# A graph-network kernel on one core: a step's five quads of edge sums spread between the other TensorE work, the first steps reordered, the looks at dst's order moved into the loop

## The chip, the cores and the metric

The kernel runs on 1 core of a Trainium2 chip. The metric is the device time in microseconds (us) of one launch; lower is better. Engines: PE is TensorE, DVE is VectorE, ACT is ScalarE, POOL is GpSimd, SP is SyncE (here it only issues DMAs).

## What is computed

12500 nodes with 128 features, 412500 edges with 48 features, sorted by receiving node dst. The reference, cut:

```python
h   = relu(layernorm(x))                                   # 12500 x 128
agg = segment_sum(edge_attr_48, dst, 12500)                # 12500 x 48
u   = graph_globals[0]                                     # 64, the same for all nodes
hid = relu(concat([h, agg, u], axis=1) @ W1 + b1)          # 12500 x 256
out = x + hid @ W2 + b2                                    # 12500 x 128
```

## The kernel before, in words

**Tiling.** Edges are read in groups of 896 (128 partitions x 7), 19 groups to a step; 24 full steps and a short one of 5 groups make 25 steps. Nodes are taken in 25 tiles of 512. Because dst is sorted, step s touches about the nodes of tile s. The 19 groups are five quads (QUADS, four groups each, the last three), in two parts: part 0 is quads 0 to 2, part 1 quads 3 and 4 (PART_QUADS).

**Sums of edges.** `make_onehot` (L795, VectorE) compares each edge's node relative to its group with a ramp of 32. `sum_quad` (L1042, TensorE) multiplies a quad's one-hots with its edges, 28 matmuls per four-group quad and pass, and leaves sums in group_bank[part]; its last matmul signals edges_used, which lets SP load the same quad of the next step (`load_quad`, L343) and VectorE make its next one-hots. `copy_sums` (ScalarE, L586) copies the sums (high part), `low_sums` (VectorE, L831) takes what is left (low part), and `place` (TensorE, L1064) places both in a window of nodes with a mask from `make_placing` (VectorE, L807). `add_window` (VectorE, L824) adds the window to agg in SBUF.

**Node network.** `moments`, `join_moments`, `invert` (VectorE, L840, L846, L853, L855) and `deviate`, `normalise` (ScalarE, L593, L601) normalise a tile of x; `turn_x` (TensorE, L1081) transposes it; `copy_turned` (ScalarE, L612) copies it. For the edge part of the first layer, `tile_high` (ScalarE, L623) copies a tile of agg and `tile_low` (GpSimd, L536) subtracts; tile s-1 is complete once part 0 of step s is added, so tile_high(s-1) waits for add_window(s, 0). `first_layer` (L1091 node, L1095 and L1097 edge matmuls) needs both; `relu_hidden` (ScalarE, L633), `second_layer` (L1108), `copy_out` (ScalarE, L641), `add_out` (GpSimd, L531) follow, the latter with `x_plus_b2` (GpSimd, L519). out_bank is used by the second layer and by turn_x in turn, hidden_bank by the first layer and by turn_rel.

**Order.** Each engine has its own program in order; semaphores join them. In step s TensorE does quads 0 to 2, second layer of tile s-2, place part 0, quads 3 and 4, turn x of tile s, first layer of tile s-1, place part 1. VectorE's and ScalarE's orders are written out in the loops of L911 and L689. GpSimd does x_plus_b2(s), tile_low(s-1), add_out(s-2). SP loads all quads of the next step, then x two tiles ahead, and every second step from 4 on stores a tile; the other stores stand at the end. All these DMAs are in one queue.

**rel.** dst is loaded in four blocks of 128 groups. `relative` (ScalarE, L562, L565) makes each row relative, `turn_rel` (TensorE, L1027) transposes it into hidden_bank, `copy_rel` (ScalarE, L574) copies it out; blocks 1 to 3 are turned in steps 2 to 4. `turn_places` (L1115) makes the positions for the masks in step 0. `sum_bias` (L1123) and `bias` (ScalarE, L671) make the hidden bias in step 1.

**The end.** `check_sorted` (VectorE, L750) looks over a block of dst for a descent, four times; `check_windows` tests the windows; a worst value decides whether a general path runs (it does not with these inputs). `last_out` (L869) adds the last two tiles.

## Time and profile before

| | us |
|---|---|
| median of 3 runs | 273.01 (272.47 to 273.25) |
| profiled execution | 272.62 |
| its span, first to last instruction | 270.9 |
| busy: PE, DVE, ACT, POOL | 243.4, 229.1, 144.7, 104.1 |
| DMA | 94.48 MB, mean 349 GB/s |

The profiled execution's time is its span and 1.7 us around it. Times in rows count from the span's start. Matmuls overlap: the starts of following groups tell the time that they take, not their busy sums, and ends of matmuls are modelled.

### The profile page before, as it was taken

Reading aid. Unit: us, or ns where it says so; the run is one execution under the profiler, and the core shown is the slowest. Engines: PE = TensorE matmul, PEld = TensorE weight load, DVE = VectorE, ACT = ScalarE, POOL = GpSimd, SP = SyncE. Lnnn points to the kernel's source line nnn. Section 1 sums busy time; section 2 is a strip of 40 time slices with the busy share of each in tenths; the row PEclk is TensorE's granted clock in tenths of the full one; section 3 lists DMA queues with packets and bytes.
Section 4 is the critical chain, followed back from the end, with each engine's and each line's share of the span. In section 5 each row is a group of like instructions: output and inputs, shape, how many; then the busy total and the mean of one; then the engine's idle time right before and its main releaser. Section 6 shows DMA issues by size and latency. Waiting matters only on the chain.

```text
span 270.9 us, 17352 instructions
## 1 busy us (share of the span) xinstructions
PE 243.4 (90%) x7438; PEld 198.7 (73%) x7438; DVE 229.1 (85%) x556; ACT 144.7 (53%) x315; POOL 104.1 (38%) x112
## 2 busy tenths in 40 slices
PE   6646599999999989999998999998999998999990
PEld 3545578878977877787786788787779678778760
DVE  1967987898999998989999899998989988985294
ACT  2644456966764555466465455536537546545540
POOL 8761033253255235225415514532532550552400
PEclk9977799999999999999999999999999999999996
DMA  7999989999999999999999999999999999999911
GB/s 242 370 359 354 341 277 374 339 328 361 341 377 377 387 384 381 367 380 382 366 385 384 388 373 371 389 382 385 381 359 364 387 382 390 362 387 322 372 48 55
DMA packets 70873, 94.48 MB, mean 349 GB/s; under 512 B 4324, under 2 KB 64260, under 8 KB 70854
## 3 DMA queue, kind: packets, MB, share of 16 engines
q1 hardware_dynamic: 69802, 94.29, 98.5%
q10 hardware_dynamic: 956, 0.00, 0.2%
q14 instruction: 15, 0.12, 0.1%
q8 instruction: 4, 0.07, 0.1%
q0 software_dynamic: 96, 0.00, 0.0%
HBM read 87.88 MB, written 6.40 MB: 348 GB/s over the span
## 4 chain that ended last, share of the span: by engine, by line
PE 46%; DMA 38%; DVE 9%; issue 3%; POOL 1%; DVEq 1%; ACT 0%; POOLq 0%
DMA edge_buf<-in_edge_attr 36%; PE group_bank L1042 18%; PE out_bank L1108 9%; PE hidden_bank L1091 8%; PE window_bank L1064 3%; DVE onehot L795 3%; PE out_bank L1081 3%; PE hidden_bank L1095 2%; PE hidden_bank L1097 2%; PE hidden_bank L1027 2%; DVE rel_rows L750 1%; DMA dst_rows<-in_dst 1%; DVE placing L807 1%; DVE bn L840 1%; DVEq L815 1%
## 5 line engine op out<-in xcount | busy, mean ns | idle before, releaser
L795 DVE TENSOR_TENSOR onehot<-rel,const_bank 128x896 f32<-128x896 f32 (+1 forms) x122 | 122.8, 1023 | 8.2 <-issue 7.9
L1042 PE MATMUL group_bank<-edge_buf,onehot 128*32 128x48 f32 x6454 | 90.2, 213 | 7.4 <-DMA edge_buf<-in_edge_attr 5.8
L1042 PEld LDWEIGHTS group_bank<-edge_buf,onehot 128*32 128x32 f32 x6454 | 81.9, 114 | 14.4 <-issue 9.8
L536 POOL TENSOR_TENSOR tile_sums<-agg,tile_sums 48x512 fp32r<-48x512 f32 x23 | 29.2, 1268 | 137.4 <-ACT tile_sums L623 137.4
L1108 PE MATMUL out_bank<-w_sb,hidden 128*128 128x128 f32 x384 | 48.5, 279 | 1.7 <-issue 0.9
L1108 PEld LDWEIGHTS out_bank<-w_sb,hidden 128*128 128x128 f32 x384 | 44.7, 191 | 4.1 <-issue 1.3
L1091 PE MATMUL hidden_bank<-normed_t,w_node 128*128 128x512 f32 (+1 forms) x100 | 46.4, 586 | 0.4 <-ACT hidden L633 0.4
L601 ACT ACTIVATE normed_x<-x_buf,shift,inverse 128x128 f32<-128x128 f32 x98 | 40.3, 494 | 2.0 <-DVE shift L855 2.0
L633 ACT ACTIVATE hidden<-hidden_bank,hidden_bias 128x512 f32<-128x512 f32 (+1 forms) x50 | 31.2, 676 | 10.7 <-PE hidden_bank L1097 10.7
L519 POOL TENSOR_TENSOR xb_buf<-x_buf,b_rows 128x512 f32<-128x512 f32 (+1 forms) x25 | 31.6, 1262 | 7.9 <-DMA x_buf<-in_x 4.7
L593 ACT ACTIVATE deviation<-mean_var,eps_col 128x4 f32<-128x4 f32 (+1 forms) x25 | 7.4, 298 | 48.3 <-DVE mean_var L846 48.3
L824 DVE TENSOR_TENSOR agg<-agg,window_bank 48x352 f32 (+1 forms) x49 | 21.6, 441 | 13.4 <-PE window_bank L1064 13.2
L531 POOL TENSOR_TENSOR out_buf<-mlp_out,xb_buf 128x512 f32<-128x512 f32 x23 | 29.3, 1275 | 5.6 <-ACT mlp_out L641 3.9
L641 ACT ACTIVATE mlp_out<-out_bank 128x512 f32<-128x512 f32 x23 | 13.7, 597 | 31.2 <-PE out_bank L1108 31.2
L1095 PE MATMUL hidden_bank<-tile_sums,w_high 112*128 112x512 f32 (+1 forms) x50 | 29.0, 581 | 0.1
L1064 PE MATMUL window_bank<-placing,sums_high 128*48 128x128 f32 (+3 forms) x122 | 23.4, 250 | 4.8 <-DVE sums_low L831 3.5
L1091 PEld LDWEIGHTS hidden_bank<-normed_t,w_node 128*128 128x128 f32 x100 | 17.0, 190 | 12.5 <-issue 12.3
L807 DVE TENSOR_TENSOR placing<-node_ramp,const_bank 128x456 fp32r<-128x456 f32 (+2 forms) x49 | 24.9, 508 | 0.0
L623 ACT ACTIVATE tile_sums<-agg 48x512 fp32r<-48x512 f32 (+1 forms) x25 | 15.6, 625 | 12.6 <-DVE agg L824 9.7
L1064 PE MATMUL window_bank<-placing,sums_low 128*48 128x128 f32 (+3 forms) x122 | 21.7, 233 | 0.0
L840 DVE BATCH_NORM_STATS2 bn<-x_buf 128x6 f32<-128x128 f32 x98 | 21.0, 271 | 0.0
L1064 PEld LDWEIGHTS window_bank<-placing,sums_high 128*48 128x48 f32 (+1 forms) x122 | 15.4, 126 | 6.5 <-issue 5.4
(97 smaller groups left out, 217.4 us busy)
## 6 DMA issues: line engine op xcount, KB each, us to landing
edge_buf<-in_edge_attr SPq DMA_DIRECT2D x97, 672.0 KB, 7.4
edge_buf<-in_edge_attr SPq DMA_DIRECT2D x24, 504.0 KB, 8.1
x_buf<-in_x SPq DMA_DIRECT2D x24, 256.0 KB, 8.3
out<-out_buf SPq DMA_DIRECT2D x23, 256.0 KB, 5.8
dst_rows<-in_dst SPq DMA_DIRECT2D x3, 448.5 KB, 6.7
dst_rows<-in_dst SPq DMA_DIRECT2D x1, 252.3 KB
out<-out_buf SPq DMA_DIRECT2D x1, 224.0 KB
edge_buf<-in_edge_attr SPq DMA_DIRECT2D x1, 168.0 KB, 5.7
```

The source lines that it names most:

```text
L519: pool.tensor_tensor(xb_buf[k.third][:, 0:nj, :], x_buf[k.parity][:, 0:nj, :], b2_rows[:, :].unsqueeze(1).to_broadcast([P, nj, F_NODE]), A ...
L531: pool.tensor_tensor(out_buf[slot(k)][:, 0:nj, :], mlp_out[:, 0:nj, :], xb_buf[k.third][:, 0:nj, :], ALU.add).then_inc(out_added, 1)
L536: pool.tensor_tensor(sums_tile(k, STACK_LOW), agg_tile(k), sums_tile(k, 0).bitcast(fp32), ALU.subtract)\
L601: done = act.activation(normed_x[:, j, :], x_buf[k.parity][:, j, :], ACT.Relu, bias=shift[:, j:j + 1], scale=inverse[:, j:j + 1])
L633: act.activation(hidden[own(k)][:, c, 0:cols], hidden_bank[c][:, 0:cols], ACT.Relu, bias=hidden_bias[:, c:c + 1]).then_inc(hidden_copied, 1)
L795: dve.tensor_tensor(onehot[:, c0:c0 + cols, :], rel[:, r0:r0 + cols].unsqueeze(2).to_broadcast([P, cols, WINDOW]), ramp_const.unsqueeze(1) ...
L807: dve.tensor_tensor(placing[h][:, 0:nq, :, 0:width], node_ramp[:, :, 0:width].unsqueeze(1).to_broadcast([P, nq, NJ, width]), position_cons ...
L1042: done = pe.matmul(group_bank[h][WINDOW * j:WINDOW * (j + 1), n * F_EDGE:(n + 1) * F_EDGE], onehot[:, (g0 + j) * EDGES_PER_ROW + r, :], ed ...
L1064: done = pe.matmul(bank[:, :, low // NJ:high // NJ], sums[h][0:rows, n, :], placing[h][0:rows, n, :, 0:(high - low) // NJ], start=(n + par ...
L1091: pe.matmul(hidden_bank[c][:, 0:cols], w1_node[:, c * P:(c + 1) * P], normed_t[own(k)][:, 0:cols], start=True, stop=False)
L1095: pe.matmul(hidden_bank[c][:, 0:cols], w1_high[:, c * P:(c + 1) * P], tile_sums[own(k)][:, 0:cols], start=False, stop=False)
L1108: done = pe.matmul(to_bank[:, j * P:(j + 1) * P], hidden[own(k)][:, c, j * P:(j + 1) * P], w2_sb[:, c, :], start=(c == 0), stop=(c == 1))
```

## The change

On TensorE a step becomes: quads 0 and 1, second layer (and in steps 1 to 3 turn_rel of block s), quads 2 and 3, turn x, place part 0, quad 4, first layer with place part 1 between its node and its edge matmuls. VectorE takes the moments ahead of part 0's low sums and part 1's low sums ahead of the fourth one-hot. ScalarE copies the result and rel ahead of part 0's sums. The first steps load x sooner, and the bias loads have a semaphore of their own; the other weights come behind the last quad of step 1. The low part of w1 is made by GpSimd. check_sorted runs in steps 10, 13, 16 and 19. Cut of the diff:

```diff
@@ -183,6 +183,7 @@
         bases_in = sem("bases_in")
         weights_in = sem("weights_in")
         b2_in = sem("b2_in")
+        bias_in = sem("bias_in")
         edges_in = [sem(f"edges_in{q}") for q in range(NQ)]
         x_in = [sem(f"x_in{p}") for p in range(2)]
         stored = [sem(f"stored{n}") for n in range(OUT_SLOTS)]
@@ -379,23 +380,23 @@
                 for row in (0, STACK_LOW):
                     sp.dma_start(w1_edge[row:row + F_EDGE, :], w1[F_NODE:F_NODE + F_EDGE, :])\
                         .then_inc(weights_in, 16)
-                sp.dma_start(w1_global[:, :], w1[F_NODE + F_EDGE:, :]).then_inc(weights_in, 16)
-                sp.dma_start(global_col[:, :], graph_globals[0:1, :].rearrange("a g -> g a")).then_inc(weights_in, 16)
-                sp.dma_start(b1_col[:, :], b1.rearrange("(c p) -> p c", p=P)).then_inc(weights_in, 16)
                 sp.dma_start(w1_node[:, :], w1[0:F_NODE, :]).then_inc(weights_in, 16)
                 sp.dma_start(w2_sb[:, :, :], w2.rearrange("(c p) n -> p c n", p=P)).then_inc(weights_in, 16)
 
             load_dst(0)
             load_part(At(0), 0)
+            load_x(At(0))
             load_part(At(0), 1)
-            load_x(At(0))
             sp.dma_start(b2_rows[:, :], bass.AP(tensor=b2.tensor, offset=0, ap=[[0, P], [1, F_NODE]]))\
               .then_inc(b2_in, 16)
             load_part(At(1), 0)
             load_x(At(1))
-            load_weights()
+            sp.dma_start(w1_global[:, :], w1[F_NODE + F_EDGE:, :]).then_inc(bias_in, 16)
+            sp.dma_start(global_col[:, :], graph_globals[0:1, :].rearrange("a g -> g a")).then_inc(bias_in, 16)
+            sp.dma_start(b1_col[:, :], b1.rearrange("(c p) -> p c", p=P)).then_inc(bias_in, 16)
             load_dst(1)
             load_part(At(1), 1)
+            load_weights()
             load_dst(2)
             load_x(At(2))
             for s in range(1, steps):
@@ -538,6 +539,12 @@
 
             for s in range(steps):
                 x_plus_b2(last_tile() if s == tiles - 1 else At(s))
+                if s == 1:
+                    pool.wait_ge(xb_ready, s + 1)
+                    pool.wait_ge(w1_high_ready, 1)
+                    pool.tensor_tensor(w1_low[:, :], w1_edge[:, :], w1_high[:, :].bitcast(fp32), ALU.subtract)\
+                        .then_inc(w1_split, 1)
+                    pool.wait_ge(w1_split, 1)
                 if 1 <= s < full_steps:
                     pool.wait_ge(xb_ready, s + 1)
                     tile_low(At(s - 1))
@@ -661,7 +668,7 @@
                    .then_inc(agg_zeroed, 1)
 
             def split_weights():
-                act.wait_ge(weights_in, 7 * 16)
+                act.wait_ge(weights_in, 4 * 16)
                 act.wait_ge(stacks_zeroed, 3)
                 act.activation(w1_high[:, :], w1_edge[:, :], ACT.Copy).then_inc(w1_high_ready, 1)
 
@@ -677,32 +684,33 @@
             act.sem_inc(turned_copied, 1)
             act.sem_inc(bias_ready, 1)
             zero_strip(2)
-            copy_sums(At(0), 0)
             zero_strip(3)
             deviate(At(0))
             normalise(At(0))
+            copy_sums(At(0), 0)
+            copy_turned(At(0))
             copy_sums(At(0), 1)
-            copy_turned(At(0))
-            split_weights()
+            bias()
+            relative(1)
             deviate(At(1))
             normalise(At(1))
             for s in range(1, full_steps):
                 following = last_tile() if s + 1 == tiles - 1 else At(s + 1)
+                if s >= 2:
+                    copy_out(At(s - 2))
+                if s < blocks:
+                    copy_rel(s)
                 copy_sums(At(s), 0)
                 if s == 1:
-                    bias()
-                if s >= 2:
-                    copy_out(At(s - 2))
-                if 2 <= s <= blocks:
-                    copy_rel(s - 1)
+                    split_weights()
                 tile_high(At(s - 1))
                 copy_sums(At(s), 1)
                 deviate(following)
                 relu_hidden(At(s - 1))
                 copy_turned(At(s))
                 normalise(following)
-                if s < blocks:
-                    relative(s)
+                if s + 1 < blocks:
+                    relative(s + 1)
                 if s == 2 * blocks:
                     load_ends(1)
             third, second, last = At(tiles - 3), At(tiles - 2), last_tile()
@@ -886,50 +894,47 @@
             for q in (3, 4):
                 make_onehot(At(0), q)
             make_onehot(At(1), 0)
-            low_sums(At(0), 0)
+            moments(At(0))
+            join_moments(At(0))
+            make_onehot(At(1), 1)
+            invert(At(0))
+            step_bases()
+            base = [window_base(At(0), h) for h in range(2)]
             dve.wait_ge(position_turned, 1)
             dve.tensor_copy(position_const.rearrange("p q s -> p (q s)"), out_bank[:, 0:NQ * steps])\
                .then_inc(position_ready, 1)
             make_placing(At(0), 0)
-            moments(At(0))
-            join_moments(At(0))
+            low_sums(At(0), 0)
             make_placing(At(0), 1)
-            make_onehot(At(1), 1)
-            invert(At(0))
-            step_bases()
-            base = [window_base(At(0), h) for h in range(2)]
             make_onehot(At(1), 2)
-            low_sums(At(0), 1)
             dve.wait_ge(agg_zeroed, 4)
             add_window(At(0), 0, base[0])
+            low_sums(At(0), 1)
             make_placing(At(1), 0)
             make_onehot(At(1), 3)
             moments(At(1))
             join_moments(At(1))
             make_onehot(At(1), 4)
             invert(At(1))
+            check_steps = [2 * blocks + 2 + 3 * b for b in range(blocks)]
             for s in range(1, full_steps):
                 n = At(s + 1)
                 add_window(At(s - 1), 1, base[1])
                 make_placing(At(s), 1)
-                if s == 1:
-                    dve.wait_ge(w1_high_ready, 1)
-                    dve.tensor_tensor(w1_low[:, :], w1_edge[:, :], w1_high[:, :].bitcast(fp32), ALU.subtract)\
-                       .then_inc(w1_split, 1)
                 if n.value * GROUPS % P + GROUPS > P:
                     dve.wait_ge(rel_ready, 2 * (n.value * GROUPS // P + 2))
                 make_onehot(n, 0)
                 base[0] = window_base(At(s), 0)
                 make_onehot(n, 1)
+                following = last_tile() if s + 1 == tiles - 1 else n
+                moments(following)
+                join_moments(following)
                 low_sums(At(s), 0)
                 make_onehot(n, 2)
                 add_window(At(s), 0, base[0])
                 make_placing(n, 0)
+                low_sums(At(s), 1)
                 make_onehot(n, 3)
-                low_sums(At(s), 1)
-                following = last_tile() if s + 1 == tiles - 1 else n
-                moments(following)
-                join_moments(following)
                 base[1] = window_base(At(s), 1)
                 make_onehot(n, 4)
                 invert(following)
@@ -938,6 +943,8 @@
                     c0 = first_last * EDGES_PER_ROW
                     link(dve.memset(rel[0:masked_rows, c0:c0 + EDGES_PER_ROW], -1.0))
                     link(dve.memset(rel[0:masked_rows + 1, c0:c0 + masked_rest], -1.0))
+                if s in check_steps:
+                    check_sorted(check_steps.index(s))
             second, last = At(tiles - 2), last_tile()
             base[0] = window_base(At(steps - 1), 0)
             add_window(At(full_steps - 1), 1, base[1])
@@ -946,8 +953,6 @@
             dve.wait_ge(tile_low_ready, tiles - 2 + 2)
             tile_low(second)
             tile_low(last)
-            for b in range(blocks):
-                check_sorted(b)
             check_windows()
             last_out(second, out_bank, tiles - 1)
             last_out(last, group_bank[0], tiles)
@@ -1081,7 +1086,7 @@
                     done = pe.transpose(to_bank[:, j * P:(j + 1) * P], normed_x[:, j, :], ident[:, :])
                 done.then_inc(x_turned, 1)
 
-            def first_layer(k):
+            def first_layer(k, between=None):
                 pe.wait_ge(w1_split, 1)
                 pe.wait_ge(bias_ready, 3)
                 pe.wait_ge(turned_copied, k.value + 2)
@@ -1090,6 +1095,8 @@
                     pe.wait_ge(hidden_copied, k.value * 2 + c + 5)
                     pe.matmul(hidden_bank[c][:, 0:cols], w1_node[:, c * P:(c + 1) * P], normed_t[own(k)][:, 0:cols],
                               start=True, stop=False)
+                if between is not None:
+                    place(between, 1)
                 pe.wait_ge(tile_low_ready, k.value + 3)
                 for c in range(2):
                     pe.matmul(hidden_bank[c][:, 0:cols], w1_high[:, c * P:(c + 1) * P], tile_sums[own(k)][:, 0:cols],
@@ -1117,7 +1124,7 @@
                 done.then_inc(position_turned, 1)
 
             def sum_bias():
-                pe.wait_ge(weights_in, 7 * 16)
+                pe.wait_ge(bias_in, 3 * 16)
                 pe.wait_ge(rel_ready, 2)
                 for c in range(2):
                     done = pe.matmul(hidden_bank[c][:, 0:1], w1_global[:, c * P:(c + 1) * P], global_col[:, :],
@@ -1140,25 +1147,31 @@
             keep_clock(4, window_bank[0])
             with pe.Fori(0, full_steps) as i:
                 step = At(0, i)
-                sum_part(step, 0)
-                with pe.If(i > blocks):
+                sum_quad(step, 0)
+                sum_quad(step, 1)
+                with pe.If(i >= blocks):
                     second_layer(step.plus(-2))
                 with pe.Else():
                     with pe.If(i > 1):
                         second_layer(step.plus(-2))
-                        turn_rel(i - 1)
+                        turn_rel(i)
                     with pe.Else():
                         with pe.If(i > 0):
-                            sum_bias()
+                            pe.wait_ge(bias_ready, 3)
+                            turn_rel(1)
                         with pe.Else():
                             turn_places()
+                sum_quad(step, 2)
+                sum_quad(step, 3)
+                turn_x(step)
                 place(step, 0)
-                sum_part(step, 1)
-                turn_x(step)
+                sum_quad(step, 4)
                 with pe.If(i > 0):
-                    pe.wait_ge(rel_ready, i * 2)
-                    first_layer(step.plus(-1))
-                place(step, 1)
+                    pe.wait_ge(rel_ready, i * 2 + 2)
+                    first_layer(step.plus(-1), step)
+                with pe.Else():
+                    sum_bias()
+                    place(At(0), 1)
 
             final, third, second, last = At(steps - 1), At(tiles - 3), At(tiles - 2), last_tile()
             sum_part(final, 0)
```

## Rows read from the trace of the kernel before

**Rows 1.** The page, GB/s moved in 40 equal slices of the span (6.8 us each).
```profile
GB/s 242 370 359 354 341 277 374 339 328 361 341 377 377 387 384 381 367 380 382 366 385 384 388 373 371 389 382 385 381 359 364 387 382 390 362 387 322 372 48 55
```
**Rows 2.** Chain of waits that ended last: start us, duration us, what.
```profile
47.92 0.24 PE window_bank L1064 x4
...
78.06 1.92 PE group_bank L1042 x168
...
82.05 0.41 PE window_bank L1064 x6
82.47 1.32 PE group_bank L1042 x98
83.79 0.59 PE out_bank L1081 x4
84.37 1.72 PE hidden_bank L1091 x4
86.09 0.23 PE hidden_bank L1095
...
87.27 1.33 PE group_bank L1042 x112
...
128.29 8.79 DMA edge_buf<-in_edge_attr
```
**Rows 3.** Timeline, from placing part 0 to tile_low, and a late first-layer matmul.
```profile
179.01 0.24 PE L1064 MATMUL window_bank<-placing,sums_low 128*48 128x152 f32 x1
...
179.39 0.52 DVE L824 TENSOR_TENSOR agg<-agg,window_bank 48x352 f32 x1 [0.52 <-PE window_bank L1064]
...
179.94 0.63 ACT L623 ACTIVATE tile_sums<-agg 48x512 fp32r<-48x512 f32 x1 [0.46 <-DVE agg L824]
...
180.71 1.27 POOL L536 TENSOR_TENSOR tile_sums<-agg,tile_sums 48x512 fp32r<-48x512 f32 x1 [5.69 <-ACT tile_sums L623]
...
257.44 1.05 DVE L861 TENSOR_TENSOR tile_sums<-agg,tile_sums 48x512 fp32r<-48x512 f32 x2 [0.76 <-ACT tile_sums L623]
...
258.21 0.50 PE L1095 MATMUL hidden_bank<-tile_sums,w_high 112*128 112x512 f32 x1
```
**Rows 4.** VectorE: timeline of a step, line L855 (ns min/median/max), and GpSimd beside it.
```profile
78.70 0.36 DVE L824 TENSOR_TENSOR agg<-agg,window_bank 48x216 f32 x1
...
83.04 0.61 DVE L807 TENSOR_TENSOR placing<-node_ramp,const_bank 128x456 fp32r<-128x456 f32 x1
...
87.92 0.37 DVE L824 TENSOR_TENSOR agg<-agg,window_bank 48x216 f32 x1
...
L855 DVE SCALAR_TENSOR_TENSOR shift<-mean_var,inverse x25: 161/732/986, 20.0 to 251.0; 128x4 f32<-128x4 f32 x24, 128x2 f32<-128x2 f32 x1
...
173.73 1.29 POOL L519 TENSOR_TENSOR xb_buf<-x_buf,b_rows 128x512 f32<-128x512 f32 x1
...
174.31 0.73 DVE L855 SCALAR_TENSOR_TENSOR shift<-mean_var,inverse 128x4 f32<-128x4 f32 x1
```
**Rows 5.** Timeline of ScalarE in steps 2 and 3, where blocks of rel are turned.
```profile
42.63 1.87 ACT L574 ACTIVATE rel<-hidden_bank 128x512 f32<-128x512 f32 x2
...
47.56 1.26 ACT L633 ACTIVATE hidden<-hidden_bank,hidden_bias 128x512 f32<-128x512 f32 x2 [0.31 <-PE hidden_bank L1097]
...
50.96 1.04 ACT L565 ACTIVATE rel_rows<-dst_rows,neg_first 128x896 f32<-128x896 int32 x1
```
**Rows 6.** Timeline of TensorE: first sums of step 2 and of the final step.
```profile
37.76 0.42 PE L1042 MATMUL group_bank<-edge_buf,onehot 128*32 128x48 f32 x20
...
252.25 1.38 PE L1042 MATMUL group_bank<-edge_buf,onehot 128*32 128x48 f32 x70
```
**Rows 7.** Timeline of the end.
```profile
258.52 1.09 DVE L750 CUSTOM_DVE_ANT_0 rel_rows<-dst_rows 128x896 f32<-128x896 int32 x1
...
263.10 1.06 PE L1108 MATMUL group_bank<-w_sb,hidden 128*128 128x128 f32 x8
...
266.67 0.41 DVE L869 TENSOR_TENSOR out_buf<-group_bank,xb_buf 128x256 f32<-128x256 f32 x1
```

## The prediction

> **What bounds it now.** I read the page's slices first, then the chain of waits, then the timeline of single steps. The slices of GB/s [rows 1] stand at 242 to 374 in the first third and near 380 from then until the loop ends: the edges come in at the best rate the run shows, and the early shortfall is made by the kernel. The chain says who holds the loop. From 78.06 to 87.27 it lies on TensorE alone: three quads of sums 1.92, then 2.07 until placing (the second layer), placing 0.41, two quads 1.32, turning x 0.59, node matmuls 1.72, four edge matmuls 0.93 (0.23 each), second placing 0.24: 9.2 us, and 9.21 by the starts [rows 2]. Later the chain has in most steps a piece such as the 8.79 us transfer, so TensorE waits for edges there; from the first sum of step 2 (37.76) to that of the final step (252.25) are 22 steps in 214.5 us, 9.75 each [rows 6]. So TensorE would need 9.2 and the transfers set about 9.7: only half a microsecond per step is hidden. VectorE is as full: 78.70 to 87.92 is 9.22 us with 0.27 idle [rows 4].
>
> **1. The loop's order on TensorE.** Removed and added work: none, but one more start of a group of sums. 168 matmuls take 1.92 and 112 take 1.33 [rows 2], so 56 cost 0.59 and a start about 0.15; the fifth quad is 1.32 - 0.15 - 0.59 = 0.58. Step: 9.21 + 0.15 = 9.36.
> What moves is the placing of part 0, and behind it hangs a chain: VectorE adds the window, ScalarE copies the tile (high), GpSimd subtracts (low), and only then may TensorE multiply by w1_high. In rows 3 placing ends at 179.24; the add starts 179.39, the copy 179.94, GpSimd 180.71 and ends 181.98: 2.74 us. A first w1_high matmul that has to wait starts 0.06 after its releaser (258.15, the 0.71 us first half of VectorE's pair at 257.44) and is itself 0.50, as at 258.21: in all 3.30 us from placing to its end. Before, two quads, the turning of x and the node matmuls cover it: 1.32 + 0.59 + 1.72 + 0.23 = 3.86 [rows 2]. After, it is the fifth quad, the node matmuls and the second placing: 0.15 + 0.58 + 1.72 + 0.24 + 0.23 = 2.92. So 0.38 us a step is a new wait: 9.36 + 0.38 = **9.74**, by the single terms 9.73. Bounds: 0, if TensorE has in truth more to do in between than its modelled ends show; 0.8, twice my value, if VectorE comes late to the add. I take 9.73, as rows 3 measure every link. That equals the old 9.75: it uses up just the slack that the transfers left. The sums released in smaller lots can keep the queue fuller, but TensorE can't use that while its own loop is 9.73. Queue order on SP is unchanged in the loop.
> Behind the second layer the copy of the result still has two quads before the turning of x. Behind the first layer the two ReLUs (1.26 us, begun 0.37 before its end at 47.93) have quads 0 and 1, 0.15 + 1.18 = 1.33 us, where they had the second placing and three quads [rows 2, 5]: nothing, and if it weren't covered, what exceeds 1.33.
>
> **2. VectorE's order.** The low part of part 1 now comes right behind the add and the placing mask, but ScalarE first copies the tile: that starts 0.55 after the add and takes 0.63 [rows 3], so its copy of sums starts 1.25 after the add and the low part, 0.3 on, 1.55 after it, while VectorE is free after add (0.52) and mask (0.61), 1.0 as they overlap [rows 3, 4]. That is 0.58 more idle. The 0.27 idle behind the moments goes, because a one-hot now covers the register load. L855 has a third effect: alone it takes 0.161, its median is 0.732, and at 174.31 it ends at 175.04, just as the GpSimd op of 173.73 ends (175.02) [rows 4]: it is held by it. In the new order it falls to the end of the GpSimd op before, some 0.3 less. VectorE's own loop: 9.2 + 0.58 - 0.27 - 0.3 = 9.2, half a microsecond under 9.73.
>
> **3. Looks at dst's order.** Four, 1.14 us from one to the next (the first at 258.52 is 1.09 long [rows 7]), in steps 10, 13, 16 and 19. Each pushes one-hots, moments and the low part of part 0, for which placing and so the whole chain of part 1 waits. Beyond the slack of 0.5 it costs about 0.7 each, 2.8 in all. Bounds: 0, if TensorE waits for edges then anyway; 1.9 each if the look is also held by a 1.28 us GpSimd op. I take 0.7, nearest to the uncontended row. The Trainium skill ("SBUF — State Buffer", section "Who interferes with whom") says that a VectorE operation with two SBUF inputs and a GpSimd one that reads SBUF exclude each other for the whole instruction. The looks have two such inputs, so the rule speaks against putting them beside GpSimd work; by it the sum would take 1.9 each wherever GpSimd is first. The trace agrees for L855.
>
> **4. Turning the rows of rel.** Before, turn_rel is 0.86 and its copies on ScalarE (1.87 [rows 5]) come after the copy of part 0's sums. After, in steps 1 to 3, they stand before it. ScalarE: first layer's end 47.93, relative's end 52.00 [rows 5], 4.07 later; then copy_out overlaps, 0.5, copy_rel 1.87, the copy of sums and the start of the low part 0.55, placing starts 0.42 later and ends 0.65 on: 8.0 after the first layer, where the plain new step has 1.33 + 2.02 + 1.33 + 0.59 + 0.41 = 5.7. So 2.3 in each of steps 2 and 3, 4.6. Bounds 0.86 (transposes alone) and 3.
>
> **5. First steps.** Step 2 begins at 37.76 [rows 6]. x comes earlier and both ScalarE fills stand together, so the first normalising ends near 18, some 3 us sooner. Against that quad 2 of step 0 waits for turn_places; its reload, and behind it on SP x of step 1, the bias loads, dst block 1 and quads 3 and 4, shift by 3 to 4 us; block 1 is then needed already in step 1. VectorE does moments, inversion and bases ahead of the position copy, placing about 2 us later but the rest sooner. I come to step 1 at 23.5 and step 2 near 36.5: -1.3. Bounds -4 (half of a step lost there comes back) and +2 (block 1 or the weights, now behind the last quad, come late). w1_low on GpSimd is 0.4 to 1 us once, in this bound.
>
> **6. The end.** Without the looks VectorE is 4.5 us earlier, but the last second-layer group of TensorE begins at 263.10 and lasts 1.06; the last addition, now at 266.67, can start at 264.25 [rows 7]: -2.4. Late next is TensorE. Bounds -1.5 and -2.6.
>
> **Sum** against the profiled execution, 272.62 us (span 270.9; the median of the runs, 273.01, is 0.4 above): loop 22 x 9.73 + 4.6 + 2.8 = 221.5 against 214.5, +7.0; start -1.3; end -2.4; together +3.3: **275.9 us**.
>
> **Rivals.** A, faster: the wait for w1_high does not show, or is shorter, the loop of TensorE is near 9.36, and delays vanish in the wait for edges. Then 22 x 9.36 + 4.6 + 2.8 = 213.3 against 214.5; with start and end -4.9, near 268; held at the transfers' rate it is 214.5 - 3.7, 268.9. I take 268.5. For it: the slices show 9.7 us of transfers per step as a floor which can also rise in rate (390 GB/s in one slice) once buffers are freed evenly; every link I add up is a modelled end. Against it: the links of rows 3 follow each other without a gap that could close. Chance 0.32.
> B, slower by more: looks held by GpSimd (1.9 each, +4.8 over the forecast), 280.7. For it: what happens to L855 [rows 4]. Against: in the new order nothing says who is first. It decides where GpSimd's addition of b2 starts before the look. Chance 0.15.
> C, no change: the new wait is 0.2, not 0.38, and half the delays are absorbed: 22 x 0.18 = 4.0 less, 272. Chance 0.10.
> The forecast has 0.43. The case on the other side is A; it decides from where placing to w1_high is ready within 2.92 us. That the change doesn't do what it says can't be: the diff only reorders.
>
> **Chances and range.** The bound for same is 0.3%, 0.8 us, about what a measurement here tells from nothing. Faster 0.33, same 0.1, slower 0.57. The forecast's own range, from the bounds of terms 1, 3 and 4, is 273.5 to 279; with A's and most of B's the range is 267.5 to 280.5.
>
> **What would show it.** Right: idle before w1_high matmuls (L1095) ended by GpSimd, near 0.4 in each step; steps of 9.7 in which waits for edges are almost gone; steps 2 and 3 near 12 us with TensorE waiting for low sums ahead of placing; steps 10, 13, 16, 19 near 10.4; the last addition 2.4 nearer to the final sums. Wrong: steps under 9.6, or waits for edges that remain, or a look of over 2 us.

## The result, and the profile after

| | before | after |
|---|---|---|
| median of 4 runs, us | 272.82 (272.47 to 273.25) | 287.38 (286.27 to 288.82) |
| profiled execution, us | 272.62 | 288.12 |
| its span, us | 270.9 | 286.2 |

The changed kernel is slower: 1.0514 times the time before, 95% interval 1.0447 to 1.0581. The forecast was 275.9 us with a range to 280.5: right in sign, far too small. The two profiled executions differ by 15.5 us, of which the forecast had 3.3. A few executions, 1.5% or more above the fastest of the same kernel, stand outside all ratios, among them one of b3 that took 469 us.

**Three stretches.** The timeline of TensorE gives the first sums of step 2 and of the final step (columns: start us, duration us, engine, line, operation, count). A step's sums of 112 matmuls are its first two quads.

```profile
39.63 1.40 PE L1047 MATMUL group_bank<-edge_buf,onehot 128*32 128x48 f32 x112
...
51.60 1.40 PE L1047 MATMUL group_bank<-edge_buf,onehot 128*32 128x48 f32 x112
...
63.27 1.40 PE L1047 MATMUL group_bank<-edge_buf,onehot 128*32 128x48 f32 x112
...
270.05 1.38 PE L1047 MATMUL group_bank<-edge_buf,onehot 128*32 128x48 f32 x70
```

| | before [rows 6] | after | difference | forecast |
|---|---|---|---|---|
| to step 2's first sums | 37.76 | 39.63 | +1.9 | -1.3 |
| 22 steps | 214.5 (9.75 each) | 230.4 (10.47 each) | +15.9 | +7.0 |
| from the final step's first sums to the end of the span | 18.65 | 16.15 | -2.5 | -2.4 |

So the end did what was forecast, the start lost where it should have gained, and most of the miss lies in the loop. Steps 2 and 3 are 11.97 and 11.67 us (39.63, 51.60, 63.27), near the 12.0 forecast; the surprise is in the plain steps. Their second layers start like this: 85.23, 95.19, 105.15 (9.96 apart), then 115.35, 126.51, 136.49, 146.97, 157.21: between 9.98 and 11.16.

**A plain step.** The chain of waits (the chain of work that ended last), after (start us, duration us, what):

```profile
85.23 2.02 PE out_bank L1115 x16
87.25 1.44 PE group_bank L1047 x111
88.69 0.59 PE out_bank L1086 x4
89.27 0.42 PE window_bank L1069 x6
89.69 0.73 PE group_bank L1047 x42
90.45 1.98 PE hidden_bank L1096 x4
...
95.19 2.02 PE out_bank L1115 x16
```

Compare with rows 2: the second layer (L1115, L1108 before), turning of x (0.59) and placing (0.42) cost what they did. The node matmuls, behind a group of sums instead of behind the turning of x, take 1.98 in the chain, not 1.72. What I had forecast as idle time, TensorE waiting for GpSimd's low part of the tile, is absent. The timeline has GpSimd's subtraction, the last matmul of the second placing and the first w1_high matmul:

```profile
111.31 1.27 POOL L537 TENSOR_TENSOR tile_sums<-agg,tile_sums 48x512 fp32r<-48x512 f32 x1 [6.15 <-ACT tile_sums L630]
...
112.57 0.22 PE L1069 MATMUL window_bank<-placing,sums_low 96*48 96x120 f32 x1
...
112.63 0.49 PE L1102 MATMUL hidden_bank<-tile_sums,w_high 112*128 112x512 f32 x1
```

GpSimd is ready at 112.58, and the w1_high matmul starts 0.06 behind the matmul before it, as those of the placing follow each other. In a plain step with the same order (a2) GpSimd is ready 0.1 ahead.

**A slow step.** Timeline from 104 to 121 us, after (in brackets the idle time before, and its releaser):

```profile
104.41 6.55 SPq L344 DMA_DIRECT2D edge_buf<-in_edge_attr  x5
...
111.06 0.68 SPq L359 DMA_DIRECT2D x_buf<-in_x  x1
...
118.77 0.87 DVE L848 BATCH_NORM_STATS2 bn<-x_buf 128x6 f32<-128x128 f32 x4 [1.83 <-DMA x_buf<-in_x]
...
119.97 0.28 DVE L839 TENSOR_TENSOR sums_low<-group_bank,sums_high 128x144 fp32r<-128x144 f32 x1
...
120.38 0.26 PE L1069 MATMUL window_bank<-placing,sums_high 128*48 128x128 f32 x1 [0.98 <-DVE sums_low L839]
```

Read it from the bottom up. TensorE stands 0.98 us before placing, for the low sums (L839); VectorE has them late because the moments (L848), which now stand ahead of them, waited 1.83 us for x; x was requested at 111.06, behind all five quads in SP's order, and the last of these requests waits for quad 4's buffer. From request to landing x took 7.68 us (chain: `111.06 7.68 DMA x_buf<-in_x`). The view of waits shows how often (us in total, times, longest us):

```profile
DVE bn L848 <- DMA x_buf<-in_x: 20.4, 19, 1.8
DVE sums_low L839 <- ACT sums_high L593: 14.3, 29, 2.3
PE window_bank L1069 <- DVE sums_low L839: 6.0, 10, 1.6
PE out_bank L1115 <- ACT normed_t L619: 4.9, 23, 0.4
```

VectorE waits for x 19 times. Before, x was asked for in the same place of SP's order, but its moments came some 3 us later in the step and no such wait showed. The wait of TensorE for edges that rows 2 showed (8.79 us transfer in the chain) is gone from the view: TensorE is now slower than the transfers. The page agrees: DMA x_buf holds 27% of the chain that ended last, and the slices of GB/s no longer stand near 380 as in rows 1:

```profile
GB/s 255 349 303 314 326 308 299 335 292 308 346 383 369 368 346 347 359 340 370 349 355 333 385 350 359 344 353 326 380 348 338 386 331 348 349 340 312 399 154 54
```

The last row of that view of waits is a wait of 0.20 in each step that no step of my prediction had: the second layer writes out_bank, which ScalarE has to have copied (turned x, L619) first, and on ScalarE that copy stands behind both ReLUs.

### The profile page after: what moved, and what is told of

It is laid out like the page before. It is cut to its first block, busy times and chain, and to the rows that moved or that the text cites. A ratio compares the mean times of both kernels' runs of the same rounds, so it can differ in the third digit from the quotient of the medians.

```text
span 286.2 us, 17374 instructions
## 1 busy us (share of the span) xinstructions
PE 258.5 (90%) x7438; PEld 200.6 (70%) x7438; DVE 227.4 (79%) x555; ACT 141.7 (50%) x315; POOL 108.0 (38%) x113
## 4 chain that ended last, share of the span: by engine, by line
PE 44%; DMA 28%; DVE 10%; ACT 8%; issue 6%; SPq 2%; ACTq 0%; DVEq 0%
DMA x_buf<-in_x 27%; PE group_bank L1047 12%; PE hidden_bank L1096 10%; PE out_bank L1115 8%; PE window_bank L1069 6%; DVE bn L848 4%; ACT hidden L640 3%; PE out_bank L1086 3%; ACT normed_t L619 3%; DVE onehot L803 2%; PE hidden_bank L1102 2%; ACT normed_x L608 2%; SPq L344 1%; PE hidden_bank L1032 1%; DVE mean_var L854 1%
## 5 line engine op out<-in xcount | busy, mean ns | idle before, releaser
L803 DVE TENSOR_TENSOR onehot<-rel,const_bank 128x896 f32<-128x896 f32 (+1 forms) x122 | 121.4, 1028 | 2.3 <-PE group_bank L1047 1.4
L1047 PE MATMUL group_bank<-edge_buf,onehot 128*32 128x48 f32 x6454 | 94.0, 212 | 1.4 <-DVE onehot L803 1.4
L1047 PEld LDWEIGHTS group_bank<-edge_buf,onehot 128*32 128x32 f32 x6454 | 83.6, 113 | 16.1 <-issue 10.5
L1115 PE MATMUL out_bank<-w_sb,hidden 128*128 128x128 f32 x384 | 48.5, 279 | 4.9 <-ACT normed_t L619 4.9
L1096 PE MATMUL hidden_bank<-normed_t,w_node 128*128 128x512 f32 (+1 forms) x100 | 50.0, 623 | 1.3 <-ACT hidden L640 0.4
L1115 PEld LDWEIGHTS out_bank<-w_sb,hidden 128*128 128x128 f32 x384 | 44.7, 191 | 7.3 <-issue 7.3
L1069 PE MATMUL window_bank<-placing,sums_high 128*48 128x128 f32 (+3 forms) x122 | 32.3, 322 | 6.3 <-DVE sums_low L839 6.0
L520 POOL TENSOR_TENSOR xb_buf<-x_buf,b_rows 128x512 f32<-128x512 f32 (+1 forms) x25 | 34.4, 1376 | 9.2 <-DMA x_buf<-in_x 6.0
L848 DVE BATCH_NORM_STATS2 bn<-x_buf 128x6 f32<-128x128 f32 x98 | 21.4, 280 | 20.5 <-DMA x_buf<-in_x 20.4
L1096 PEld LDWEIGHTS hidden_bank<-normed_t,w_node 128*128 128x128 f32 x100 | 17.2, 192 | 16.8 <-issue 16.6
L1069 PEld LDWEIGHTS window_bank<-placing,sums_high 128*48 128x48 f32 (+1 forms) x122 | 15.2, 127 | 15.9 <-issue 15.7
L839 DVE TENSOR_TENSOR sums_low<-group_bank,sums_high 128x96 fp32r<-128x96 f32 (+1 forms) x49 | 13.2, 270 | 14.3 <-ACT sums_high L593 14.3
L1102 PE MATMUL hidden_bank<-tile_sums,w_high 112*128 112x512 f32 (+1 forms) x50 | 21.7, 435 | 0.1
```

What stands on the lines that cost most here:

```text
L520: pool.tensor_tensor(xb_buf[k.third][:, 0:nj, :], x_buf[k.parity][:, 0:nj, :], b2_rows[:, :].unsqueeze(1).to_broadcast([P, nj, F_NODE]), A ...
L803: dve.tensor_tensor(onehot[:, c0:c0 + cols, :], rel[:, r0:r0 + cols].unsqueeze(2).to_broadcast([P, cols, WINDOW]), ramp_const.unsqueeze(1) ...
L848: dve.bn_stats(bn6[:, j, :], x_buf[k.parity][:, j, :]).then_inc(moments_halfway, 1)
L1047: done = pe.matmul(group_bank[h][WINDOW * j:WINDOW * (j + 1), n * F_EDGE:(n + 1) * F_EDGE], onehot[:, (g0 + j) * EDGES_PER_ROW + r, :], ed ...
L1069: done = pe.matmul(bank[:, :, low // NJ:high // NJ], sums[h][0:rows, n, :], placing[h][0:rows, n, :, 0:(high - low) // NJ], start=(n + par ...
L1096: pe.matmul(hidden_bank[c][:, 0:cols], w1_node[:, c * P:(c + 1) * P], normed_t[own(k)][:, 0:cols], start=True, stop=False)
```

## The experiments

Each was timed beside the kernel before. "After with" and "before with" say which kernel was edited. Ratios are to the kernel before.

### Late x

Theory: x's landing, through VectorE's order, is most of the loop's miss. Rival: the wait is cover for something else that is late anyway. Two ways to remove it: put the moments back (a1), or ask for x sooner (a2).

**a1**, after with the moments back behind part 1's low sums:

```diff
-                following = last_tile() if s + 1 == tiles - 1 else n
-                moments(following)
-                join_moments(following)
                 low_sums(At(s), 0)
...
                 make_onehot(n, 3)
+                following = last_tile() if s + 1 == tiles - 1 else n
+                moments(following)
+                join_moments(following)
```

> The changed kernel, with VectorE's moments of the next tile put back behind part 1's low sums, as in the kernel before; nothing else. Theory X (the moments, moved some 3 us ahead in the step, wait for x to land, and part 0's low sums and placing wait behind them; 20.4 us of such waits in the changed kernel): the waits of the moments for x fall from 20.4 us to under 2, steps of over 10.3 us vanish except those with a look, and the time falls by 6 to 8 us, to about 280. Theory P (the new order on TensorE sets the step, the moments' wait is hidden beside it): the waits go but the time stays within 2 us of 287.

Measured: 289.23 us, ratio 1.0551 (1.0482 to 1.0620): no gain. **a2**, after with x asked for behind quad 1:

```diff
-                if s + 1 < steps:
-                    load_part(At(s + 1), 0)
-                    load_part(At(s + 1), 1)
+                quads = range(len(quads_of(At(s + 1)))) if s + 1 < steps else ()
+                for q in quads[:2]:
+                    load_quad(At(s + 1), q)
                 if s + 2 < tiles:
                     load_x(last_tile() if s + 2 == tiles - 1 else At(s + 2))
+                for q in quads[2:]:
+                    load_quad(At(s + 1), q)
```

> The changed kernel, with x of two tiles ahead requested by SP behind quad 1 instead of behind quad 4; VectorE's order stays. Theory X: x lands about 3 us sooner, the moments' waits go, and the time falls as much as with the moments put back, 6 to 8 us, to about 280. Theory P: under 2 us. A third view, that the early moments are bad for VectorE's order even with x there (they stand ahead of part 0's low sums): a smaller fall than with the moments put back, by 2 us or more.

Measured: 281.08 us (280.57 to 282.01), ratio 1.0246 (1.0178 to 1.0315), 6.3 us below the changed kernel. The waits for x are gone but one, in step 1, and the plain steps are 9.96 us throughout (second layers at 85.43, 95.39, 105.34). The 22 steps take 223.6 us (first sums at 40.29 and 263.88) instead of 230.4. So late x in the loop cost 6.3 us by the medians and 6.8 by the traces, and 9.96 is what is left of the plain step without it.

Why a1 gained nothing is in its waits:

```profile
ACT deviation L600 <- DVE mean_var L854: 59.2, 25, 2.5
...
PE out_bank L1115 <- ACT normed_t L619: 16.6, 23, 0.8
```

The waits for x are gone there too. But in ScalarE's order `deviate` stands ahead of the ReLUs and the copy of turned x. With the moments late it stops ScalarE for 2.5 us (after: one such wait, 2.2), so the copy is late and the second layer waits 0.7 on average where it waited 0.2 (16.6 and 4.9 us in 23); the timeline of ScalarE in a1 has the chain in three rows:

```profile
124.17 0.30 ACT L600 ACTIVATE deviation<-mean_var,eps_col 128x4 f32<-128x4 f32 x1 [2.52 <-DVE mean_var L854]
124.37 1.25 ACT L640 ACTIVATE hidden<-hidden_bank,hidden_bias 128x512 f32<-128x512 f32 x2
125.51 0.59 ACT L619 ACTIVATE normed_t<-out_bank 128x512 f32<-128x512 f32 x1
```

Its plain steps are all 10.50 us. In this TensorE order the moments must be early for ScalarE, and x must be earlier still; the change moved the first and left the second.

### The plain step of 9.96

**a4**, after with quad 2 ahead of the second layer, which gives ScalarE 0.6 us more for the copy of turned x:

```diff
                 sum_quad(step, 1)
+                sum_quad(step, 2)
...
-                sum_quad(step, 2)
                 sum_quad(step, 3)
```

> The changed kernel, with quad 2 ahead of the second layer again (three quads, second layer, one quad, turning of x, placing, quad 4). Theory N (the second layer waits for the copy of the turned x, 0.2 us a step, because it stands only two quads behind the first layer; and part 0's sums are ready late): the wait of the second layer for normed_t goes and a plain step falls from 9.96 to about 9.75, and placing waits less behind late low sums; 3 to 5 us faster. Theory X alone: no more than 1 us, since what a step waits for is x.

Measured: 284.78 us (282.37 to 286.45), ratio 1.0374 (1.0272 to 1.0477), 2.6 us below the changed kernel. The wait for the turned x is gone, but the turning of x, with one quad instead of two behind the second layer, now waits: 0.16 on average in 20 steps, and 2.4 once. The view names no releaser; by the order of the semaphores I take it to be the copy of the result out of the same bank (not shown), which ScalarE makes from 97.86 to 98.46 in the step whose turning starts, late, at 98.72:

```profile
PE out_bank L1086 <- issue: 5.5, 21, 2.4
```

Its undisturbed steps are 9.88 to 9.95 us: the wait moved with the bank. The waits for x remain (15.8 us in 17).

**c2**, a2 with placing and quad 4 ahead of the turning of x, so that 0.59 us more lie between placing and the w1_high matmuls:

```diff
-                turn_x(step)
                 place(step, 0)
                 sum_quad(step, 4)
+                turn_x(step)
```

> The changed kernel with x requested behind quad 1 (281.1 us; all plain steps 9.96), and placing and quad 4 ahead of the turning of x. That gives the chain from placing to w1_high 0.59 us more cover, and takes 0.59 from the low sums ahead of placing. If the prediction's step 1 holds (0.38 us a step of waiting for w1_high): plain steps near 9.6 and 4 to 8 us faster. If the wait is small and the step's 9.96 is TensorE's own work and its switches between sums and full-width matmuls: 9.9 to 10.2, the same or 1 to 5 us slower, for the low sums.

Measured: 282.04 us (280.28 to 282.22), ratio 1.0311 (1.0274 to 1.0347): not below a2. The steps are 9.97 still. So the wait for w1_high, the 0.38 of my step 1, is not what makes the plain step long. c2 alone would be a weak proof, for TensorE now waits a little for the low sums ahead of placing (0.26 in four of its steps); but in its trace GpSimd is ready 0.36 ahead of the w1_high matmul, which starts 0.06 behind the placing all the same.

**d1**, before with quad 4 behind the turning of x: one more group of sums, and nothing else, in the kernel before:

```diff
-                sum_part(step, 1)
+                sum_quad(step, 3)
                 turn_x(step)
+                sum_quad(step, 4)
```

> The kernel before, with quad 4 behind the turning of x: one more group of sums between full-width matmuls, as the changed kernel has. The steps that TensorE alone sets (9.21 us between 70.8 and 89.5) measure what one more switch costs. The prediction's step 1 has 0.15 us: 9.36. The changed kernel's chain suggests about 0.5 (a node matmul group of 1.98 behind sums, 1.72 behind the turning of x): 9.7. In the loop's rest the edges hide most of either: the time grows by 0 to 2 us by the first, 2 to 5 by the second.

Measured: 278.16 us (277.07 to 278.62), ratio 1.0154 (1.0112 to 1.0195). Its timeline, of TensorE from 107 us:

```profile
107.23 0.80 PE L1042 MATMUL group_bank<-edge_buf,onehot 128*32 128x48 f32 x56
107.97 0.66 PE L1081 MATMUL out_bank<-ident,normed_x 128*128 128x128 f32 x4
108.55 0.80 PE L1042 MATMUL group_bank<-edge_buf,onehot 128*32 128x48 f32 x42
109.38 1.98 PE L1091 MATMUL hidden_bank<-normed_t,w_node 128*128 128x512 f32 x4
110.80 0.80 PE L1095 MATMUL hidden_bank<-tile_sums,w_high 112*128 112x512 f32 x1
```

and the same work in the kernel before:

```profile
111.50 1.39 PE L1042 MATMUL group_bank<-edge_buf,onehot 128*32 128x48 f32 x98
112.82 0.65 PE L1081 MATMUL out_bank<-ident,normed_x 128*128 128x128 f32 x4
113.31 1.88 PE L1091 MATMUL hidden_bank<-normed_t,w_node 128*128 128x512 f32 x4
114.63 0.80 PE L1095 MATMUL hidden_bank<-tile_sums,w_high 112*128 112x512 f32 x1
```

By the starts: 107.23 to 110.80 is 3.57 us, 111.50 to 114.63 is 3.13. One more group of sums costs 0.44 us, with no wait in it, and the steps that wait for no edges are 9.64 us long (75.14 to 84.78 from second layer to second layer), 0.43 above 9.21. My 0.15 was the part of it that lies inside the group; the rest shows in the neighbours, whose first matmul starts later on either side of a group of sums.

But in d1's loop little of it shows, because TensorE had been waiting for the transfers: from 75.14 to 250.50 are 18 steps in 175.4 us, and in the kernel before 18 steps from 70.81 to 245.08 in 174.3. The waits for edges, 5.8 us in 11 places before, are 0.6 in 2. The other 4 us of d1 lie in its first steps. The three from the second layer of step 2 take 32.06 us instead of 30.73, 0.44 more each: there no wait for edges hides the price. The second layer of step 2 itself starts at 43.08 instead of 40.08. Part of that are matmuls that take longer (turning x 1.12 us at 34.96, 0.66 in the kernel before at 34.28); the rest I haven't taken apart.

### The turning of rel

**b1**, a2 with the blocks of rel turned in steps 2 to 4, and copied behind part 0's sums, as before:

```diff
-                if s < blocks:
-                    copy_rel(s)
                 copy_sums(At(s), 0)
+                if 2 <= s <= blocks:
+                    copy_rel(s - 1)
...
-                        turn_rel(i)
+                        turn_rel(i - 1)
```

> The changed kernel with x requested behind quad 1 (281.1 us), and in it the rows of rel turned as in the kernel before: blocks 1 to 3 in steps 2 to 4, made relative one step ahead, copied behind part 0's sums. The changed kernel's steps 2 and 3 take about 12 us for a plain 9.96. If ScalarE's copies ahead of part 0's sums and the late relative are the cost (the prediction's step 4, 2.3 a step), steps 2 to 4 fall to about 10.9 and step 1 shortens too: 2 to 3 us faster, near 278.5. If the copies only move to the way of tile_high, where the new order has no cover (placing to w1_high), steps 2 to 4 stay near 12 and the time is the same or 1 us more.

Measured: 282.92 us (280.59 to 283.67; the fastest is the profiled one), ratio 1.0371 (1.0335 to 1.0407), no better than a2. Its three steps of turning are 11.7 us each (first sums at 37.56, 49.23, 60.89, 72.55). TensorE stands ahead of the turning in it and in the changed kernel alike. The timelines, of b1 and then of the changed kernel:

```profile
53.42 1.13 PE L1033 MATMUL hidden_bank<-ident,rel_rows 128*128 128x128 f32 x7 [0.46 <-ACT rel_rows L574]
```

```profile
43.84 1.13 PE L1032 MATMUL hidden_bank<-ident,rel_rows 128*128 128x128 f32 x7 [0.47 <-ACT rel_rows L572]
```

From the turning to the sums behind it are 1.06 us in b1 (54.48 is their start). With 0.46 of waiting that is 1.5 of the 1.7 that such a step has over 9.96. What I had named, the copies of rel ahead of the copy of sums on ScalarE, would make TensorE wait at the placing; three turns at 1.7 cost more than after's two at 2.0 and 1.7 and a third in step 1, so the old order of the copies gains nothing.

### The looks

**a3**, after with the four looks back at the end:

```diff
-                if s in check_steps:
-                    check_sorted(check_steps.index(s))
...
+            for b in range(blocks):
+                check_sorted(b)
             check_windows()
```

> The changed kernel with the four looks at dst's order back at the end. The look costs 0.7 us each in the loop by the prediction's step 3, and saves 2.4 at the end: the loop gets 2.8 us shorter, the end 2.4 longer, so the time stays within 1 us of 287. If a look costs the step all of its 1.1 us and more (1.9 by the rival in which GpSimd holds it): 3 to 5 us faster than the changed kernel. If looks are hidden behind the wait for x: 2 us slower than it.

Measured: 288.73 us (286.19 to 292.59), ratio 1.0481 (1.0401 to 1.0561): can't be told from the changed kernel. **b2** does the reverse, before with the looks in steps 10, 13, 16 and 19:

```diff
+                if s in check_steps:
+                    check_sorted(check_steps.index(s))
...
-            for b in range(blocks):
-                check_sorted(b)
             check_windows()
```

> The kernel before, with only the four looks moved into steps 10, 13, 16 and 19. There VectorE has half a microsecond of slack a step. Theory L (a look is hidden where the edges set the step): 2.4 us faster than before, the saving at the end, near 271. The prediction's step 3 (0.7 us each on the loop): 0.4 us slower to the same. The rival with GpSimd's hold (1.9 each): 5 us slower.

Measured: 270.71 us (270.03 to 271.87), ratio 0.9917 (0.9888 to 0.9946): faster by 2.1 us, nearly the 2.4 of my step 6. In the kernel before the looks cost nothing in the loop. **b3**, before with the looks in VectorE's waits of the last two steps (two behind one-hots of the last full step, two around the low sums of the final step):

```diff
                 make_onehot(n, 2)
+                if s == full_steps - 1:
+                    check_sorted(0)
                 add_window(At(s), 0, base[0])
...
                 make_onehot(n, 4)
+                if s == full_steps - 1:
+                    check_sorted(1)
                 invert(following)
...
             add_window(At(full_steps - 1), 1, base[1])
+            check_sorted(2)
             low_sums(At(steps - 1), 0)
+            check_sorted(3)
             add_window(At(steps - 1), 0, base[0])
```

> The kernel before, with the four looks in VectorE's waits of the last two steps, where no one-hots are left to make (waits of 1.35, 0.74, 1.56 and 1.51 us stand there). If they fit, the loop is untouched and the end 2.4 us shorter: 2 to 2.5 us faster than before. If a look that doesn't fit delays the window's addition on which the last first layers hang, the gain is only 1 to 1.5.

Measured: 271.49 us, ratio 0.9948 (0.9915 to 0.9980): a gain too, but not more than b2's.

In a2, where little else varies, the steps behind a look are 10.10 to 10.12 against 9.96: 0.15 each, 0.6 in all. And there the trace has a look beside GpSimd's addition of b2:

```profile
163.90 1.08 DVE L760 CUSTOM_DVE_ANT_0 rel_rows<-dst_rows 128x896 f32<-128x896 int32 x1
164.10 2.02 POOL L522 TENSOR_TENSOR xb_buf<-x_buf,b_rows 128x512 f32<-128x512 f32 x1
```

The look was first and kept its 1.08; GpSimd's operation, 1.28 elsewhere, took 2.02. It was held by the look, and nobody waited for it.

### The first steps

**b4**, before with the whole of after's first steps: the order of the loads, of ScalarE and VectorE until step 1, w1_low on GpSimd. Its VectorE part:

```diff
-            low_sums(At(0), 0)
+            moments(At(0))
+            join_moments(At(0))
+            make_onehot(At(1), 1)
+            invert(At(0))
+            step_bases()
+            base = [window_base(At(0), h) for h in range(2)]
             dve.wait_ge(position_turned, 1)
...
             make_placing(At(0), 0)
+            low_sums(At(0), 0)
```

> The kernel before, with only the changed first steps (order of the first loads, ScalarE's and VectorE's order ahead of the loop, w1's low part on GpSimd); loop, looks and turning of rel as before. The prediction's step 5 has it 1.3 us faster in step 2's start; the changed kernel's own trace has it 1.9 later, but there turning of rel in step 1 is in it. If that turning is the cost: 0 to 1.5 us faster than before. If the late loads of quads, block 1 and weights are: 1 to 3 us slower.

Measured: 276.52 us (275.74 to 276.96), ratio 1.0128 (1.0093 to 1.0163): 3.7 us lost. **c3**, before with the order of the loads and w1_low on GpSimd alone (of b4, without the engines' order):

```diff
             load_part(At(0), 0)
+            load_x(At(0))
             load_part(At(0), 1)
-            load_x(At(0))
...
-            load_weights()
             load_dst(1)
             load_part(At(1), 1)
+            load_weights()
```

> The kernel before, with only the changed order of the first loads (x of tile 0 ahead of part 1, bias loads with a semaphore of their own, the other weights behind the last quad of step 1) and w1's low part on GpSimd; ScalarE's and VectorE's first steps as before. With their order changed too it was 3.7 us slower, TensorE waiting 4.3 us for the low sums ahead of the first placing. If the loads are the cause: the same 3 to 4 us slower. If the engines' order is: within 1 us of before.

Measured: 273.09 us, ratio 0.9974 (0.9942 to 1.0007): no difference. So the loss of b4 is in the engines' order. The timeline of b4:

```profile
16.21 0.73 PE L1118 MATMUL out_bank<-ident,spread 25*128 25x25 f32 x5 [3.45 <-issue]
16.62 1.25 POOL L520 TENSOR_TENSOR xb_buf<-x_buf,b_rows 128x512 f32<-128x512 f32 x1
16.65 1.30 DVE L770 TENSOR_TENSOR step_base_f<-step_base_i,base_floor 1x50 f32<-1x50 int32 x1
...
19.94 0.30 DVE L903 COPY const_bank<-out_bank 128x125 f32<-128x125 f32 x1 [1.57 <-issue]
...
21.25 0.34 PE L1067 MATMUL window_bank<-placing,sums_high 128*48 128x128 f32 x1 [4.32 <-DVE sums_low L838]
```

and of the kernel before:

```profile
16.38 0.30 DVE L891 COPY const_bank<-out_bank 128x125 f32<-128x125 f32 x1 [2.25 <-PE out_bank L1115]
...
17.59 0.33 PE L1064 MATMUL window_bank<-placing,sums_high 128*48 128x128 f32 x1 [1.25 <-DVE placing L807]
...
20.04 0.19 DVE L763 TENSOR_TENSOR step_base_f<-step_base_i,base_floor 1x50 f32<-1x50 int32 x1
```

The positions are ready on TensorE at about the same time (group starting 16.21, 15.86 before). Before, VectorE was already waiting for them; in b4 it is at the bases, a chain of small operations that ends in reads of registers. The first is 1.30 us long (0.19 before), because it falls beside GpSimd's 1.25; then 1.57 pass without an instruction. The copy comes at 19.94 instead of 16.38 and placing at 21.25 instead of 17.59: 3.7 us, as much as the whole loss. At the second layer of step 2 the two traces are 2.7 apart (42.78, 40.08). A single trace is not exact there: b2 and b3, whose first steps are those of the kernel before, have that layer at 41.48 and 40.59.

The changed kernel has the same late placing (21.28), and so has a1. But a1 begins step 2 at 36.40, where I had put it (near 36.5), and the changed kernel at 39.63. What lies between is in step 1, in the timelines of the changed kernel and then of a1:

```profile
31.85 0.87 DVE L848 BATCH_NORM_STATS2 bn<-x_buf 128x6 f32<-128x128 f32 x4 [1.16 <-DMA x_buf<-in_x]
...
33.46 0.26 PE L1069 MATMUL window_bank<-placing,sums_high 128*48 128x128 f32 x1 [1.57 <-DVE sums_low L839]
...
34.84 3.35 PE L1096 MATMUL hidden_bank<-normed_t,w_node 128*128 128x512 f32 x4
```

```profile
31.83 0.26 PE L1069 MATMUL window_bank<-placing,sums_high 128*48 128x128 f32 x1 [0.62 <-DVE sums_low L839]
...
33.22 1.98 PE L1096 MATMUL hidden_bank<-normed_t,w_node 128*128 128x512 f32 x4
...
36.40 1.40 PE L1047 MATMUL group_bank<-edge_buf,onehot 128*32 128x48 f32 x112
```

It is the same fault as in the loop: the moments of tile 2 wait for x (chain: `26.99 4.83 DMA x_buf<-in_x`), the low sums stand behind them, and TensorE waits for those. Then its node matmuls take 3.35 us instead of 1.98, at a granted clock of 0.50, the lower of its two levels, between 36 and 38 us (a1 has 1.00 there). A later landing of the hidden bias's load, 1.1 us, is a smaller part. Four other kernels with the early moments wait for x of tile 2 too, and TensorE with them: a2 3.31, a3 3.30, a4 3.34 and b1 2.57 us; a2's new order begins in the loop and leaves this x, requested ahead of it, where it was.

**c1**, b2 with the low sums sooner in steps 0 and 1, since b2's view of waits had TensorE waiting for them in five places (5.1 us):

```diff
+            low_sums(At(0), 1)
             step_bases()
...
-            low_sums(At(0), 1)
...
+                if s == 1:
+                    low_sums(At(s), 0)
                 base[0] = window_base(At(s), 0)
                 make_onehot(n, 1)
-                low_sums(At(s), 0)
+                if s > 1:
+                    low_sums(At(s), 0)
```

> The kernel before with the looks in its loop (270.7 us), and VectorE's low sums sooner in the two places of the first steps where TensorE waits for them in the kernel before: part 1's of step 0 ahead of the step bases and their register loads (TensorE waits 1.11 us there), part 0's of step 1 one one-hot sooner (2.42 us). If what is gained in the first steps lasts until the edges set the step (the kernel before lets the edges in at 277 to 361 GB/s until 75 us, 380 after): 1.5 to 2.5 us faster, near 268.5. If the gain is taken back at the first wait for edges: the same as 270.7.

Measured: 272.14 us (271.45 to 273.27), ratio 0.9978 (0.9951 to 1.0005): no gain, rather worse than b2. Its waits still have 6.1 us in four places: the one ahead of part 1's placing in step 0 is gone, but the one in step 1 grew from 2.7 to 4.4 us. At the low sums that I moved ahead, VectorE waits 1.85 us for ScalarE's copy, and all that stands behind comes later.

The best version is b2, at 0.9917 of the kernel before.

## Why the prediction was wrong

**Step 1, the loop's order: terms mis-sized, the size of the step 0.23 too small.** I forecast 9.36 of work and 0.38 of wait for w1_high, 9.73. Measured are 9.96: the work is 9.21 plus 0.44 for one more group of sums (d1), and 0.20 of wait for the turned x: 9.85. The last 0.11 I can't assign. The wait for w1_high is nothing: GpSimd is ready 2.76 us behind the placing's end (109.82 and 112.58; I had 2.74), and TensorE gets there 2.81 behind it. The 0.15 for a group came from a fit inside groups (168 against 112 matmuls) and left out what the neighbours lose. So the links were right and the cover was too short: the node matmuls take 1.98 in the chain, not 1.72, and I had counted the w1_high matmul with 0.50, as if late, against 0.23. The wait that did come was named nowhere: I counted only the ReLUs between the first layer and the next second layer, at "nothing", and forgot that the copy of the turned x stands behind them and shares a bank with the second layer. The claim that the transfers absorb a TensorE loop of up to 9.7 held nearly, in d1 (9.64, 1.1 us lost in 18 steps). Above it every hundredth counts: 20 plain steps at 0.23 are 4.6 us of the miss.

**Step 2, VectorE's order: the step that failed.** I found nothing late in having the moments early and gave 9.2 for VectorE's loop. I had noted that SP's order in the loop is unchanged, and didn't ask when x lands in it. It is requested behind quad 4, takes about 7 us and is then late for moments that come 3 us sooner; behind the moments stand the low sums, and TensorE waits for them. In the loop that is 6.3 us by the medians, 6.8 by the traces (a2); in step 1 it comes once more, under step 5.

**Step 3, the looks: too dear.** Forecast 2.8, measured 0.6 in a2 and nothing in b2. The lower of my two bounds was the near one: VectorE had most of the room. As to GpSimd, rows 4 and the two new cases show the mutual hold both ways: L522 took 2.02 instead of 1.28 behind a look, L770 took 1.30 instead of 0.19 behind GpSimd. The Trainium skill ("SBUF — State Buffer", section "Who interferes with whom") says that the one that starts first keeps the ports for the whole instruction and the other blocks fully. The trace agrees in both directions. It hurt in b4, where the held operation was VectorE's, on the way to the first placing.

**Step 4, turning rel: right in size, not in its reason.** 11.97 and 11.67 us, forecast 9.73 + 2.3. But of the reason little is left: with the copies behind part 0's sums (b1) the steps are 11.7 still. It is the turning itself (1.06, where I took its 0.86 as a lower bound) and a wait of 0.46 for `relative`, which I had not priced.

**Step 5, the first steps: wrong sign, within its bounds.** Forecast -1.3, measured +1.9. I had placing "about 2 us later but the rest sooner". It was 3.7 later, and in the TensorE order of the kernel before 2.7 of them are left at step 2 (b4). In the new order they are made up for: a1 has the same late placing and begins step 2 at 36.40, 1.4 us sooner than the kernel before. So the steps that I had added up came out; what I had left out is x once more, now that of tile 2, for which the early moments wait in step 1, and the lower clock behind that wait. That rests on single traces, but five kernels with the early moments show the wait, and a1, which has them late, doesn't.

**Step 6, the end: right.** -2.4 forecast, -2.5 in the trace, and 2.1 when done alone (b2).

**The sum.** 4.6 (plain step), 6.8 (late x in the loop), -2.2 (looks), -0.4 (turning rel, 23.6 against 24.1 for the two steps), 3.2 (first steps) and -0.1 (end) are 11.9 of the 12.2 us between the forecast and the profiled execution. Of the rivals, A rested on the right point, that the wait for w1_high does not show, but its step of 9.36 didn't follow: the price of the fifth group and the wait for turned x took its place. C's step, 9.55, is excluded by 9.96 as well. B was nearest in time, for a reason that the runs exclude.

**The signs.** Of those named for "right", the waits for edges are gone, steps 2 and 3 are near 12 us, and the last addition is 2.2 nearer to the final sums (12.2 us, before 14.4; forecast 2.4). The waits ahead of w1_high are absent, and TensorE waits ahead of the turning of rel and not of the placing. None of those named for "wrong" came up, though the forecast was: nothing in my list looked at x.

## What to carry to other kernels

When an operation is moved forward on one engine, ask for each of its inputs when it arrives, DMAs included, and what stands behind it on its engine: an early read of a late transfer stops everything behind it. And an order that spreads work in smaller lots pays for each change between kinds of matmul; take the price of a change from starts on both sides of it, not from the length of the lot. Work that only has to be done some time (here four looks, 1.1 us each) can be nearly free on an engine that has room in the loop (nothing in b2, 0.15 each in a2), where at the end it cost 2.1 to 2.5 us in all.

## What the hardware showed that I had not expected

One more change between 32-column sums and full-width matmuls took 0.44 us (3.57 against 3.13 us for the same instructions), though the rows show no idle time in it. Of that I had seen 0.15. The whole step agrees: 9.64 for 9.21, and 10.77 for 10.32 where rel is turned.

A VectorE operation on 50 elements of one partition took 1.30 us instead of 0.19, as it fell beside a GpSimd operation of 1.25: here the price of the meeting went by the other's length, not by its own.

A 256 KB load of x, requested behind full quads, landed 6.9 us after its request in the changed kernel (median of 24; 7.68 at 111.06), and a quad of 672 KB after 6.5 (median of 97). Its size did not make it faster; that the requests ahead of it set the time is my reading, and no run here tests it alone.
